# Spreading a rotary rotation over the next product's row tiles in the opening stage of an attention kernel

## The chip, the cores and the metric

The kernel runs on one core of a Trainium2 chip. The metric is the device time of one execution in microseconds (us); the time before is the median of three runs. TensorE (PE) multiplies matrices into PSUM, VectorE (DVE), ScalarE (ACT) and GpSimd (POOL) work on the results, and SyncE (SP) issues transfers. Each engine takes its own instructions in order and waits on semaphores.

## The reference, cut to what matters

For x of 1024 tokens by 512 channels:

```
xn = layernorm(x)
q, k, v = xn@wq + bq, xn@wk + bk, xn@wv + bv          # 32 query heads, 8 key/value heads, 16 wide
q, k = rope(q), rope(k)                                # rotary positions
s = softmax(q k^T / 4) v                               # each key/value head serves 4 query heads
z = xn@W^T + b;  m = sum_e p_e * (xn@A_e)@B_e          # dense part and low-rank part
gamma = min(0.5*|z| / (|m| + 1e-6), 1)
out = x + s * silu(z + gamma*m)
```

## The kernel before, in words

**Groups.** The attention runs as eight groups, one for each key/value head with its four query heads. The softmax subtracts a row maximum from each row of scores, so the maxima of group g+1 are found while group g is computed: in a group PE alternates a score tile for ACT's exponential (line 1501) with a row tile of the next group (`score_rows`, line 1369), and DVE reduces each row tile to its maximum (`row_max`, line 1081; 64 reductions in a group, 448 in all). Row tiles go round four PSUM banks (`sm`); tile n waits until DVE has read tile n-4. Every third score is followed by a block of P times V (line 1469), or, at the start of group 0, by half of a dense product (`dense3`, line 1442).

**The opening stage.** Group 0's own maxima come from 32 row tiles, numbered 0 to 31 here, each of two matmuls into two banks (`next_maximum`, line 1394). For each, ACT takes the relu of one bank (`first_relu`, line 849) and DVE adds the other and takes the maximum (`first_row_max`, line 1069). A tile waits until DVE has done the row maximum of the tile before the last (two banks each). These tiles are mixed into twelve products, in the order of the list `MIXED` (line 69): q(1,0), v1, q(1,1), u0, q(2,0), u1, q(2,1), z0, q(3,0), z1, q(3,1), z2, with the number of row tiles in each. Most products have two halves of six matmuls (line 1248); up to two row tiles stand after each half. Low-rank products m0 to m3 (line 1277) go ahead of the z. The loops of PE (line 1400), DVE (line 1126) and ACT (line 899) all walk `MIXED`.

**A rotation.** A query product q is rotated in five steps: DVE multiplies by the cosine (line 1047), exchanges the pairs of rows (the shuffle, line 1049) and multiplies by the sine (line 1051), in `rope`; POOL adds the two (`rope_sum`, line 591); ACT makes the high part (`cast`, line 820) and POOL the low part (`low_part`, line 595), which SP then puts in place. Before, DVE does its three after all the row maxima of that q, and ACT the cast ahead of the third relu of the next product (`r == 2`).

**Who frees a bank.** The products go round four banks, in the order of the list `PJ`; a product waits until the one four places before it has been read (`claim`, line 1223). A q's bank is free after its shuffle; a z's after DVE's `add_b` (line 1123); q(3,0) takes the bank of q(2,1). At the start of group 0 the first score takes the bank of q(3,1), and `dense3` the bank of z2 (`claim_bank`, lines 1439 and 1498).

**Other work of the stage.** ACT squares m and z for their norms (lines 865 and 876), POOL computes gamma (line 661), DVE adds gamma*m to z (`gate_sum`, line 1095), ACT takes the tanh (line 853) and DVE finishes the gate (`gate`, line 1101). ACT's `square_of_m(3)` waits for `gate(0)`. High and low parts of W^T, A and B are made by ACT, DVE (line 1110) and POOL on the way.

Of the kernel before, what the change touches and what calls it, by code (L numbers as in the profile page):

```python
# [23 lines left out]
F32 = mybir.dt.float32  # L24
# [5 lines left out]
P = 128  # L30
# [38 lines left out]
MIXED = [("q", (1, 0), 4), ("v", 1, 0), ("q", (1, 1), 4), ("u", 0, 3), ("q", (2, 0), 3), ("u", 1, 3), ("q", (2, 1), 3),  # L69
         ("z", 0, 3), ("q", (3, 0), 2), ("z", 1, 2), ("q", (3, 1), 2), ("z", 2, 3)]  # L70
# [8 lines left out]

for _kind, _i, _rows in MIXED:  # L80
    if _kind == "z":
        PJ += [("m", _i, "act")] + ([("m", _i + 1, "act")] if _i == 2 else [])
    PJ += [(_kind, _i, "act" if (_kind, _i) == ("u", 1) else "dve")]
    if (_kind, _i) == ("z", 0):
        PJ += [("max0", 0, "act")]
# [102 lines left out]
def build(nc, x, wq, wk, wv, biases, bv, wT, b, A, B, p_sc, cosT, sinT, ident, identb, ones, out):  # L188
    ctx = ExitStack()
    with ctx:  # L190
# [354 lines left out]
        def _(pool):  # L545
# [72 lines left out]

            rope_sum(0)
            for n in range(len(halves) - 2):  # L620
                low_part(n)
# [15 lines left out]
                if halves[n] == ("q", (1, 1)):  # L637
                    for k, c in enumerate((0, 1)):
                        pool.wait_ge(wT_high_done, 3 + k)
                        pool.tensor_tensor(by_columns(wT_low_parts[:, c, :]), by_columns(wT_sb[:, c, :]),  # L640
                                           wT_high(c).bitcast(F32), ALU.subtract).then_inc(wT_low_pool, 1)
                    pool.wait_ge(b_high_done, 1)
                    pool.tensor_tensor(b_low[:, :], B_sb[:, :], b_high[:, :].bitcast(F32),
                                       ALU.subtract).then_inc(b_low_done, 1)
# [13 lines left out]
            def gamma(t):  # L658

                pool.wait_ge(norm_done, 2 * t + (3 if t == 2 else 2))  # L660
                pool.tensor_tensor(gam[:, t, :], norms[:, t, :], consts[:, 1:2].broadcast_to((P, 2)),  # L661
                                   ALU.pow).then_inc(pow_step, 1)
                pool.wait_ge(pow_step, 4 * t + 1)
                pool.tensor_scalar(gam[:, t, 1:2], gam[:, t, 1:2], EPS_M, None, ALU.add).then_inc(pow_step, 1)
                pool.wait_ge(pow_step, 4 * t + 2)
                pool.tensor_tensor(gam[:, t, 1:2], gam[:, t, 1:2], consts[:, 2:3], ALU.pow).then_inc(pow_step, 1)
                pool.wait_ge(pow_step, 4 * t + 3)
                pool.tensor_tensor(gam[:, t, 0:1], gam[:, t, 0:1], gam[:, t, 1:2], ALU.mult).then_inc(pow_step, 1)
                pool.wait_ge(pow_step, 4 * t + 4)
                pool.tensor_scalar(gam[:, t, 0:1], gam[:, t, 0:1], C_CLAMP, 1.0, ALU.mult,  # L670
                                   ALU.min).then_inc(gamma_done, 1)

# [8 lines left out]
            gamma(0)  # L681
# [3 lines left out]
            pool.wait_ge(pj_dve, emptied(PJ_AT["v", 1])[1])  # L685
# [111 lines left out]
        def _(act):  # L797
# [100 lines left out]
            entry, waiting = 0, None  # L898
            for kind, i, rows in MIXED:
                if kind == "v":  # L900
                    cast(waiting)
                    waiting = None
# [3 lines left out]
                for r in range(rows):  # L906
                    if r == 2 and waiting is not None:
                        cast(waiting)
                        waiting = None
# [107 lines left out]
        def _(dve):  # L1017
# [17 lines left out]
            def rope(kind, i):  # L1035
# [647 lines left out]
```

## Time and profile before

| | |
|---|---|
| median of 3 runs | 427.78 us (427.43 to 428.59) |
| the profiled execution | 427.93 us, span 426.1 us, mean granted clock 0.986 |
| busy, share of the span | PE 96%, DVE 84%, ACT 78%, POOL 44% |
| opening stage with row tiles | about 36 to 97 us |
| groups 0 to 6 | 97 to about 375 us |
| last group and end | to 426 us |

A busy PE is no proof of a PE bound: its matmuls are pipelined, their ends are modelled, and PE can be paced by whoever empties its banks. So the views below are read for who waits for whom, and for the starts of instructions rather than for their ends.

### The profile page before, as it was taken

How to read it: one execution, taken by the hardware profiler on the slowest of the kernel's cores; microseconds unless marked ns; L12 is line 12 of the kernel's file. 1: busy time of each engine (PE TensorE's matmuls, PEld its weight loads, DVE VectorE, ACT ScalarE, POOL GpSimd, SP SyncE). 2: the span in 40 equal slices, each digit the busy share in tenths (PEclk: the TensorE clock that was granted, in tenths of full speed). 3: DMA queues.
4: the chain of work that ended last, by engine and by line, in shares of the span. 5: the costliest groups of instructions: out<-in, count | busy, mean ns of one | idle time of the engine just before them, and what ended most of it. 6: DMA issues, size and time to landing. Idle time of an engine off the chain costs nothing.

```text
span 426.1 us, 8603 instructions
## 1 busy us (share of the span) xinstructions
PE 410.3 (96%) x3215; PEld 195.0 (46%) x3215; DVE 356.6 (84%) x643; ACT 333.6 (78%) x653; POOL 189.2 (44%) x243
## 2 busy tenths in 40 slices
PE   7999989989999999999999999999999999999994
PEld 3556545655434344444444443444444343454441
DVE  5862677775999999999999999999999999933553
ACT  2445354574899998999989898999999999976884
POOL 7979972548444230403142043314332455501555
PEclk9999999995999999999999999999999999999999
DMA  8959995544610020000000000000000030002002
GB/s 263 306 119 127 130 135 75 77 75 75 190 37 3 0 58 3 3 3 0 3 2 4 1 3 3 2 4 0 4 2 3 1 102 2 4 2 88 25 22 68
DMA packets 15449, 21.51 MB, mean 50 GB/s; under 512 B 3328, under 2 KB 7712, under 8 KB 15408
## 3 DMA queue, kind: packets, MB, share of 16 engines
q1 hardware_dynamic: 13888, 19.85, 22.6%
q10 hardware_dynamic: 1520, 1.12, 1.0%
q8 instruction: 25, 0.41, 0.4%
q14 instruction: 16, 0.13, 0.1%
HBM read 10.13 MB, written 2.10 MB: 29 GB/s over the span
## 4 chain that ended last, share of the span: by engine, by line
PE 84%; POOL 6%; ACT 4%; DVE 3%; issue 2%; DMA 1%; DVEq 0%; ACTq 0%; POOLq 0%
PE st L1501 33%; PE oT L1469 27%; PE oT L1556 3%; PE sm L1581 3%; PE st L1248 2%; PE sm L1478 2%; PE oT L1248 2%; PE st L1535 2%; PE sm L1394 2%; PE sm L1369 1%; POOL arena L591 1%; PE oT L1442 1%; POOL x_low_parts L602 1%; DVE relus L1069 1%; POOL qA L595 1%
## 5 line engine op out<-in xcount | busy, mean ns | idle before, releaser
L1081 DVE TENSOR_REDUCE half_top<-sm 128x1 f32<-128x512 f32 x448 | 271.0, 680 | 4.2 <-PE sm L1369 3.6
L979 ACT ACTIVATE arena<-st 128x512 f32<-128x512 f32 x448 | 233.0, 600 | 25.4 <-PE st L1501 20.5
L1369 PE MATMUL sm<-kA,qA 48*128 48x512 f32 x448 | 157.4, 446 | 1.4 <-DVE row_top L1069 1.4
L1501 PE MATMUL st<-qA,kA 50*128 50x512 f32 x448 | 155.3, 442 | 0.1
L1469 PE MATMUL oT<-arena,vg 128*32 128x256 f32 (+3 forms) x1568 | 128.5, 419 | 0.1
L1501 PEld LDWEIGHTS st<-qA,kA 50*128 50x128 f32 x448 | 74.0, 186 | 97.7 <-ACT arena L979 80.8
L718 POOL TENSOR_TENSOR rsum<-junk,consts 128x16 f32<-128x16 f32 x13 | 37.9, 2915 | 101.2 <-ACT junk L947 101.2
L1369 PEld LDWEIGHTS sm<-kA,qA 48*128 48x128 f32 x448 | 74.0, 186 | 3.2 <-DVE row_top L1069 2.1
L1469 PEld LDWEIGHTS oT<-arena,vg 128*32 128x32 f32 x1568 | 33.5, 108 | 46.1 <-issue 42.5
L1069 DVE CUSTOM_DVE_ANT_0 relus<-sm,relus 128x512 f32<-128x512 f32 x32 | 21.4, 687 | 19.9 <-ACT relus L849 16.3
L1004 ACT ACTIVATE arena<-st 128x512 f32<-128x512 f32 x48 | 26.9, 601 | 9.4 <-PE st L1535 9.4
L613 POOL TENSOR_TENSOR maxp<-row_top,consts 128x16 bf16<-128x16 f32 x16 | 3.5, 216 | 60.9 <-DVE row_top L1088 60.9
L849 ACT ACTIVATE relus<-sm 128x512 f32<-128x512 f32 x32 | 18.0, 594 | 12.8 <-PE sm L1394 12.8
L1394 PE MATMUL sm<-k_first,qA 48*128 48x512 f32 x64 | 13.7, 469 | 4.1 <-DVE row_top L1069 3.9
L661 POOL TENSOR_TENSOR gam<-norms,consts 128x2 f32<-128x2 f32 x8 | 5.7, 715 | 26.9 <-DVE uT L1194 21.5
L591 POOL TENSOR_TENSOR arena<-arena 128x512 f32<-128x512 f32 x9 | 11.5, 1276 | 12.9 <-DVE arena L1051 12.9
L1556 PE MATMUL oT<-arena,vg 128*32 128x512 f32 x128 | 15.6, 599 | 1.0 <-ACT arena L1004 1.0
L820 ACT ACTIVATE arena<-arena 128x512 fp32r<-128x512 f32 x7 | 4.4, 629 | 13.2 <-POOL arena L591 13.2
L1535 PE MATMUL st<-qA,kA 50*128 50x512 f32 x48 | 12.7, 464 | 0.1
L1186 DVE TENSOR_TENSOR late_gate<-sm,b_sb 128x512 f32<-128x512 f32 x4 | 2.8, 692 | 11.2 <-PE sm L1581 11.2
L1394 PEld LDWEIGHTS sm<-k_first,qA 48*128 48x128 f32 x64 | 5.4, 184 | 14.2 <-DVE row_top L1069 7.7
L595 POOL TENSOR_TENSOR arena<-arena 128x512 fp32r<-128x512 f32 x7 | 9.0, 1286 | 5.5 <-ACT arena L820 5.5
(193 smaller groups left out, 483.0 us busy)
## 6 DMA issues: line engine op xcount, KB each, us to landing
qA<-arena SPq DMA_DIRECT2D x45, 128.0 KB, 4.6
x_sb<-in_x SPq DMA_DIRECT2D x16, 256.0 KB, 3.8
wT_sb<-in_wT SPq DMA_DIRECT2D x2, 1024.0 KB, 7.0
kA<-qA SPq DMA_DIRECT2D x12, 128.0 KB, 6.7
out<-x_sb SPq DMA_DIRECT2D x1, 896.0 KB, 4.3
out<-x_sb SPq DMA_DIRECT2D x4, 224.0 KB, 2.0
z_sb<-in_wq SPq DMA_DIRECT2D x1, 768.0 KB, 10.0
B_sb<-in_B SPq DMA_DIRECT2D x2, 256.0 KB, 7.1
```

What stands on the lines that cost most here:

```text
L718: pool.tensor_tensor(sums, came[:, :, :, D], consts[:, 2:3].unsqueeze(2).broadcast_to((P, TH, REP)), ALU.pow).then_inc(sums_inv, 1)
L849: act.activation(relus[:, e % 2, :], sm[:, 2 * e % 4, :], ACT.Relu).then_inc(relu_done, 1)
L979: act.activation(probs[:, s % PB, h, :], st[:, st_score(0, s, h) % 3, :], ACT.Exp, scale=float(D) ** -0.5).then_inc(st_free, 1)
L1004: act.activation(probs[:, s % PB, h, :], last_bank(last_score(s, k)), ACT.Exp, scale=float(D) ** -0.5).then_inc(last_free, 1)
L1069: return dve.tensor_tensor_reduce(relus[:, n % 2, :], bank, relus[:, n % 2, :], 1.0, LOWEST, ALU.add, ALU.max, to)
L1081: dve.tensor_reduce(half_top[:, e // 16, e % 16, j % 2:j % 2 + 1], sm[:, n % 4, :], AX.X, ALU.max).then_inc(sm_free, count)
L1369: pe.matmul(sm[:, n % 4, :], qA[rows, half, g // 2, h, qt * P:(qt + 1) * P], kA[rows, g // 2, kh * HALF:(kh + 1) * HALF], start=True, stop ...
L1394: pe.matmul(sm[:, n % 4, :], queries, k_first[kh * ROWS:kh * ROWS + KR, :], start=True, stop=True).then_inc(sm_full, 1)
L1469: mm = pe.matmul(oT[h * VC:(h + 1) * VC, cols], vg[:, g % 2, kt, :], probs[:, (NT * half + kt) % PB, h, cols], start=(kt == 0), stop=(kt = ...
L1501: pe.matmul(st[:, n % 3, :], kA[rows, g // 2, kt * P:(kt + 1) * P], qA[rows, half, g // 2, h, :], start=True, stop=True).then_inc(st_full, 1)
L1535: pe.matmul(last_bank(n), kA[rows, place, kt * P:(kt + 1) * P], qA[rows, half, place, h, :], start=True, stop=True).then_inc(last_full, 1)
L1556: mm = pe.matmul(oT[h * VC:(h + 1) * VC, :], vg[:, LAST % 2, s % NT, :], probs[:, s % PB, h, :], start=(s % NT == 0), stop=(s % NT == NT - 1))
```

## The change

Two row tiles move to the front: u0 and u1 get four instead of three, q(3,1) one instead of two and z2 two instead of three. DVE's three instructions of a rotation now stand in the next product of `MIXED`: the cosine after its first row maximum, the shuffle after its second, the sine after its third; what does not fit (fewer row tiles) follows its last row maximum. The rotation of q(1,0) stands in v1, which has no row tiles, as before. ACT's cast moves behind the relus of the product after that. The reading of v1's bank moves from DVE to ACT. DVE's `gate_sum(1)` and `add_b(2)` move from between the row maxima of z2 to behind the rotation of q(3,1). On POOL the low parts of W^T and B go ahead of `low_part` of q(1,1), and `gamma(0)` ahead of `low_part` of q(2,1).

```diff
-MIXED = [("q", (1, 0), 4), ("v", 1, 0), ("q", (1, 1), 4), ("u", 0, 3), ("q", (2, 0), 3), ("u", 1, 3), ("q", (2, 1), 3),
-         ("z", 0, 3), ("q", (3, 0), 2), ("z", 1, 2), ("q", (3, 1), 2), ("z", 2, 3)]
+MIXED = [("q", (1, 0), 4), ("v", 1, 0), ("q", (1, 1), 4), ("u", 0, 4), ("q", (2, 0), 3), ("u", 1, 4), ("q", (2, 1), 3),
+         ("z", 0, 3), ("q", (3, 0), 2), ("z", 1, 2), ("q", (3, 1), 1), ("z", 2, 2)]
...
-    PJ += [(_kind, _i, "act" if (_kind, _i) == ("u", 1) else "dve")]
+    PJ += [(_kind, _i, "act" if (_kind, _i) in (("u", 1), ("v", 1)) else "dve")]
...
             for n in range(len(halves) - 2):
+                if halves[n] == ("q", (2, 1)):
+                    gamma(0)
+                if halves[n] == ("q", (1, 1)):
+                    for k, c in enumerate((0, 1)):
...
                 low_part(n)
...
-            gamma(0)
             split(len(halves) - 2)
             gamma(1)
             split(len(halves) - 1)
-            pool.wait_ge(pj_dve, emptied(PJ_AT["v", 1])[1])
+            pool.wait_ge(pj_dve, emptied(PJ_AT["v", 0])[1])
+            pool.wait_ge(pj_act, emptied(PJ_AT["v", 1])[1])
...
-            entry, waiting = 0, None
+            entry, turning, waiting = 0, None, None
             for kind, i, rows in MIXED:
                 if kind == "v":
-                    cast(waiting)
-                    waiting = None
+                    act.wait_ge(pj_full, PJ_AT["v", i] + 1)
+                    act.activation(v_sb[:, i * TH:(i + 1) * TH, :],
+                                   pj(PJ_AT["v", i]).rearrange("p (t n) -> p t n", t=TH), ACT.Copy).then_inc(pj_act, 1)
+                    cast(turning)
+                    turning = None
...
                 for r in range(rows):
-                    if r == 2 and waiting is not None:
-                        cast(waiting)
-                        waiting = None
...
-                if kind == "q":
-                    waiting = halves.index((kind, i))
-                elif waiting is not None:
+                if waiting is not None:
                     cast(waiting)
-                    waiting = None
+                waiting = turning
+                turning = halves.index((kind, i)) if kind == "q" else None
...
+            cast(waiting)
...
-            def rope(kind, i):
+            def rope(kind, i, stages=range(3)):
...
-            gate_work = {("z", 1, 0): (gate_sum, 0), ("q", (3, 1), 0): (gate, 0), ("z", 2, 0): (gate_sum, 1)}
+            gate_work = {("z", 1, 0): (gate_sum, 0), ("q", (3, 1), 0): (gate, 0)}
...
-            n = 0
+            n, turning = 0, None
             for kind, i, rows in MIXED:
...
                 for r in range(rows):
-                    if (kind, i, r) == ("z", 2, 2):
-                        add_b(2)
                     first_row_max(n)
                     n += 1
+                    if turning is not None and r < 3:
+                        rope("q", turning, (r,))
...
-                if kind == "q":
-                    rope("q", i)
+                if turning is not None and rows < 3:
+                    rope("q", turning, range(rows, 3))
+                turning = i if kind == "q" else None
                 if (kind, i) == ("u", 0):
                     low_of_u()
-                if kind == "v":
-                    keep_values(i)
-                if kind == "z" and i != 2:
+                if kind == "z":
+                    if i == 2:
+                        gate_sum(1)
                     add_b(i)
```

## Rows read from the trace of the kernel before

**Rows 1.** The page's costliest groups: DVE's reductions of groups 0 to 6

```profile
L1081 DVE TENSOR_REDUCE half_top<-sm 128x1 f32<-128x512 f32 x448 | 271.0, 680 | 4.2 <-PE sm L1369 3.6
```

**Rows 2.** Timeline of DVE, 94 to 163 us (start, duration, engine, line, operation)

```profile
94.14 1.38 DVE L1095 SCALAR_TENSOR_TENSOR z_sb<-m_sb,gam,z_sb 128x512 f32<-128x512 f32 x1
...
96.05 0.68 DVE L1123 TENSOR_TENSOR z_sb<-oT,b_sb 128x512 f32<-128x512 f32 x1
...
97.26 1.87 DVE L1081 TENSOR_REDUCE half_top<-sm 128x1 f32<-128x512 f32 x3
101.83 1.89 DVE L1081 TENSOR_REDUCE half_top<-sm 128x1 f32<-128x512 f32 x3 [2.70 <-PE sm L1369]
105.51 0.69 DVE L1174 TENSOR_TENSOR z_sb<-oT,b_sb 128x512 f32<-128x512 f32 x1 [1.79 <-PE oT L1442]
106.27 1.89 DVE L1081 TENSOR_REDUCE half_top<-sm 128x1 f32<-128x512 f32 x3
...
143.46 19.33 DVE L1081 TENSOR_REDUCE half_top<-sm 128x1 f32<-128x512 f32 x32
```

**Rows 3.** Busy time by 1 us stretches: PE, PEld, DVE, ACT, POOL; granted clock; DMA

```profile
96.00:97.00 1.00, 0.73 (x4) 0.30 (x4) 1.00 (x4) 0.86 (x3) 1.00 (x2) 0.93 0.06 23
97.00:98.00 1.00, 0.61 (x1) 0.28 (x1) 1.00 (x4) 1.00 (x3) 0.84 (x3) 0.50 0.69 209
...
107.00:108.00 1.00, 1.00 (x11) 0.26 (x9) 1.00 (x2) 0.81 (x2) 0.00 (x0) 0.95 0.00 0
```

**Rows 4.** Waits of PE, 36 to 106 us: total, times, longest

```profile
PE sm L1394 <- DVE row_top L1069: 3.9, 5, 1.2
```

**Rows 5.** Timeline of PE in the opening stage: row tiles and halves of products

```profile
66.37 0.49 PE L1394 MATMUL sm<-k_first,qA 48*128 48x512 f32 x2 [0.53 <-DVE row_top L1069]
...
71.07 0.51 PE L1394 MATMUL sm<-k_first,qA 48*128 48x512 f32 x2
...
72.30 0.40 PE L1248 MATMUL oT<-wq_high,x_high_parts 128*128 128x512 f32 x1
...
73.76 0.73 PE L1394 MATMUL sm<-k_first,qA 48*128 48x512 f32 x4
74.42 0.50 PE L1248 MATMUL oT<-wT_high,x_high_parts 128*128 128x512 f32 x1
...
76.01 0.51 PE L1394 MATMUL sm<-k_first,qA 48*128 48x512 f32 x2
...
91.47 0.73 PE L1394 MATMUL sm<-k_first,qA 48*128 48x512 f32 x4
```

**Rows 6.** Timeline of DVE in the opening stage

```profile
45.44 0.68 DVE L1062 COPY v_sb<-st 128x512 f32<-128x512 f32 x1
49.20 0.69 DVE L1069 CUSTOM_DVE_ANT_0 relus<-sm,relus 128x512 f32<-128x512 f32 x1 [3.08 <-ACT relus L849]
...
65.53 0.68 DVE L1069 CUSTOM_DVE_ANT_0 relus<-sm,relus 128x512 f32<-128x512 f32 x1
...
72.38 0.69 DVE L1069 CUSTOM_DVE_ANT_0 relus<-sm,relus 128x512 f32<-128x512 f32 x1 [1.33 <-ACT relus L849]
...
72.99 0.74 DVE L1047 SCALAR_TENSOR_TENSOR arena<-st,bias,arena 128x512 f32<-128x512 f32 x1
...
74.43 0.75 DVE L1051 SCALAR_TENSOR_TENSOR arena<-arena,bias 128x512 f32<-128x512 f32 x1
```

**Rows 7.** Timeline of ACT in the opening stage

```profile
71.61 0.60 ACT L849 ACTIVATE relus<-sm 128x512 f32<-128x512 f32 x1 [1.43 <-PE sm L1394]
...
90.27 0.60 ACT L865 ACTIVATE junk<-st 128x512 bf16<-128x512 f32 x1 [0.36 <-PE st L1277]
...
92.39 1.10 ACT L849 ACTIVATE relus<-sm 128x512 f32<-128x512 f32 x2
```

**Rows 8.** Timeline of POOL, 93 to 97 us: sum and low part of q(3,1)

```profile
93.70 1.27 POOL L591 TENSOR_TENSOR arena<-arena 128x512 f32<-128x512 f32 x1 [2.39 <-DVE arena L1051]
95.71 1.28 POOL L595 TENSOR_TENSOR arena<-arena 128x512 fp32r<-128x512 f32 x1 [0.74 <-ACT arena L820]
```

More of the change, by code:

```diff
@@ L617, in maxima, with gamma @@
                                    ALU.subtract).then_inc(max_parts, 1)
+            def gamma(t):
+                pool.wait_ge(norm_done, 2 * t + (3 if t == 2 else 2))
+                pool.tensor_tensor(gam[:, t, :], norms[:, t, :], consts[:, 1:2].broadcast_to((P, 2)),
+                                   ALU.pow).then_inc(pow_step, 1)
+                pool.wait_ge(pow_step, 4 * t + 1)
+                pool.tensor_scalar(gam[:, t, 1:2], gam[:, t, 1:2], EPS_M, None, ALU.add).then_inc(pow_step, 1)
+                pool.wait_ge(pow_step, 4 * t + 2)
+                pool.tensor_tensor(gam[:, t, 1:2], gam[:, t, 1:2], consts[:, 2:3], ALU.pow).then_inc(pow_step, 1)
+                pool.wait_ge(pow_step, 4 * t + 3)
+                pool.tensor_tensor(gam[:, t, 0:1], gam[:, t, 0:1], gam[:, t, 1:2], ALU.mult).then_inc(pow_step, 1)
+                pool.wait_ge(pow_step, 4 * t + 4)
+                pool.tensor_scalar(gam[:, t, 0:1], gam[:, t, 0:1], C_CLAMP, 1.0, ALU.mult,
+                                   ALU.min).then_inc(gamma_done, 1)
             rope_sum(0)
             for n in range(len(halves) - 2):
+                if halves[n] == ("q", (2, 1)):
+                    gamma(0)
+                if halves[n] == ("q", (1, 1)):
+                    for k, c in enumerate((0, 1)):
+                        pool.wait_ge(wT_high_done, 3 + k)
+                        pool.tensor_tensor(by_columns(wT_low_parts[:, c, :]), by_columns(wT_sb[:, c, :]),
+                                           wT_high(c).bitcast(F32), ALU.subtract).then_inc(wT_low_pool, 1)
+                    pool.wait_ge(b_high_done, 1)
+                    pool.tensor_tensor(b_low[:, :], B_sb[:, :], b_high[:, :].bitcast(F32),
+                                       ALU.subtract).then_inc(b_low_done, 1)
                 low_part(n)
@@ L636, in _ @@
                     low_of_tokens(1)
[L637 to L644, printed above, removed]
                 if halves[n] == ("q", (2, 0)):
@@ L656, in split @@
                 low_part(n)
[L658 to L671, printed above, removed]
             def group_values(g):
@@ L1041, in rope @@
                 tok = slice(hh * HALF, (hh + 1) * HALF)
-                dve.wait_ge(pj_full, e + 1)
-                if n >= 2:
-                    dve.wait_ge(part2, n - 1)
-                if n == 4:
-                    dve.wait_ge(diff_done, 1)
-                dve.scalar_tensor_tensor(rotated_at(n), pj(e), bias[:, col, 0:1], cos_sb[:, tok],
-                                         ALU.add, ALU.mult).then_inc(cos_mul, 1)
-                dve.stream_shuffle(swp[:, n % 2, :], pj(e), PARTNER).then_inc(pj_dve, 1)
-                dve.wait_ge(pj_dve, emptied(e)[1])
-                dve.scalar_tensor_tensor(swp[:, n % 2, :], swp[:, n % 2, :], bias[:, col, 1:2], sin_sb[:, tok],
-                                         ALU.add, ALU.mult).then_inc(sin_mul, 1)
+                if 0 in stages:
+                    dve.wait_ge(pj_full, e + 1)
+                    if n >= 2:
+                        dve.wait_ge(part2, n - 1)
+                    if n == 4:
+                        dve.wait_ge(diff_done, 1)
+                    dve.scalar_tensor_tensor(rotated_at(n), pj(e), bias[:, col, 0:1], cos_sb[:, tok],
+                                             ALU.add, ALU.mult).then_inc(cos_mul, 1)
+                if 1 in stages:
+                    dve.stream_shuffle(swp[:, n % 2, :], pj(e), PARTNER).then_inc(pj_dve, 1)
+                if 2 in stages:
+                    dve.wait_ge(pj_dve, emptied(e)[1])
+                    dve.scalar_tensor_tensor(swp[:, n % 2, :], swp[:, n % 2, :], bias[:, col, 1:2], sin_sb[:, tok],
+                                             ALU.add, ALU.mult).then_inc(sin_mul, 1)
             dve.wait_ge(small_in, 64)
```

## The prediction

> **What bounds the kernel now.** Read first the page's costliest groups: DVE's 448 reductions stand idle for 4.2 us in all [rows 1]. In the middle of the run 32 of them take 19.33 us without a gap, 0.604 us each [rows 2]. So from the first reduction to the last, DVE sets the pace; PE looks busy because it waits in line for DVE's banks. What happens before counts by two things: when this train of reductions starts (97.26), and the gaps in its first 10 us. These are 2.70 and 1.79 us [rows 2], the first when PE computes the first half of `dense3`, the second when DVE waits for its second half. I take as yardstick the seventh reduction, at 106.27 [rows 2]; what it is shifted by, the end is shifted by.
>
> Then the granted clock: 2.4 GHz up to 96, 0.93 of it in the stretch to 97, 0.50 (the 1.2 GHz level) from 97 to 107 and back at 107 to 108 [rows 3]. PE's busy share ahead of the fall was 0.73 and 0.61 of a stretch, with waits for row maxima between [rows 3]. That is why the two halves of `dense3` leave DVE idle.
>
> Last the waits of the opening stage: row tiles waited five times for a row maximum, 3.9 us in all, 1.2 at the longest [rows 4].
>
> **Prices.** From one profiled execution: a row maximum occupies DVE 0.61 us (72.38 to 72.99), cosine and shuffle together 1.44 (72.99 to 74.43), so 0.67 and 0.77, and the sine 0.67 like the cosine [rows 6]. A row maximum can start 1.31 us after its tile (71.07 to 72.38), 0.77 of it after the start of its relu (71.61) [rows 5 to 7]. A waiting tile starts 0.84 after the row maximum that lets it go (65.53 to 66.37) [rows 5, 6]. Half a product takes 1.46 us after another matmul (72.30 to 73.76) and 1.59 after row tiles (74.42 to 76.01); two row tiles take 0.66, one about 0.45 [rows 5]. Two squares of m with their copies hold ACT 2.12 us (90.27 to 92.39) [rows 7]. A POOL sum takes 1.27 us and the low part can start 0.74 after it [rows 8].
>
> **Part 1: v1's copy goes to ACT.** Worth nothing. DVE made it at 45.44, and then stood idle for 3.08 us until a relu at ACT; ACT had been waiting for a cast [rows 6]. The Trainium skill (Perfetto Trace Analysis, Optimizing Scalar/DVE Operations) says that moving work from DVE to ScalarE may pay where DVE is saturated; by it the sum would be 0.7 us lower. DVE isn't saturated there, so the row decides.
>
> **Part 2: u0 to q(2,1), rotations between row tiles.** I replayed the new orders of PE, DVE and ACT with the prices above, from tile 7 on (nothing before it changes). Row maximum 8 no longer waits for a whole rotation, so tile 10 starts at 54.9 rather than after the longest of those waits (1.2). But row maximum 9 now stands behind the cosine, and tile 11 waits 0.8 us for it. Tile 13 waits for row maximum 11, which has shuffle, sine and a low part of W^T ahead of it: 1.0. The same twice more around u1, where DVE's row maxima 15 to 18, the rotation and the second low part of W^T are one unbroken stretch of 5.2 us: tile 18 waits 0.9, tile 20 1.05. Together 3.75 us, where about 2.6 of the old 3.9 us lie in this stretch (one wait lies ahead of it, one in z2) [rows 4], and some 0.4 more inside pairs of tiles. So the waits move and don't shrink. z0's first row tile starts at 74.65; before, at 73.76 [rows 5]. It is 0.9 us later, with two more tiles done. The two tiles that are then missing further down save 0.66 us as a pair and about 0.9 apart [rows 5], so this part alone is about even.
>
> **Part 3: q(3,0) waits for a bank.** It takes the bank of q(2,1), free after the shuffle. Before, the shuffle was done ahead of z0's row maxima. Now it follows row maximum 23: that is row maximum 22 at 75.95, cosine, row maximum 23, shuffle from 77.8 to 78.6. PE has finished z0 and the transposed maxima by 77.5, and waits 1.15 us. Everything behind it in PE's order (m1, z1) waits too. `add_b(0)` comes after the sine, at 79.9, so ACT's square of z0 and the relus behind it go late, which makes DVE idle but doesn't hold PE again.
>
> **Part 4: z1 to z2.** z1's first tile at 84.6, q(3,1)'s at 88.35, z2's first tile at 93.2; before 91.47 with one tile fewer done [rows 5], so 1.7 us later. `gate_sum(0)` meets no POOL operation now and takes about 0.75 us like the sine; `gate_sum(1)` took 1.38 because POOL's sum had started at 93.70, ahead of it at 94.14 [rows 2, 6, 8]. On the other side, `gate(0)` after row maximum 29 now starts just behind POOL's low part of q(3,0), which follows the cast that ACT makes behind relu 29. I count about 1 us for it, since the bounds are 0 and a whole 1.28 [rows 8] and the replay has POOL first by only 0.2. ACT's square of m3 waits for that gate, and relu 30 for both squares: 95.4 rather than 94.4.
>
> **Part 5: the end of the stage.** Before, the train of reductions followed the last row maximum at once; `gate_sum(1)` and `add_b(2)` were done earlier [rows 2]. Now row maximum 30 is at 96.15, cosine, row maximum 31 at 97.45, shuffle at 98.05, sine at 98.8, `gate_sum(1)` at 99.5, `add_b(2)` at 100.15: the train starts at **100.8, 3.5 us later**. PE finishes z2 at 95.5 and then waits for q(3,1)'s shuffle, whose bank the first score takes, until 98.9. It does three scores with their row tiles (0.7 us) and waits again until 100.85 for `add_b(2)`, whose bank `dense3` takes. ACT's exponentials stand behind the last cast, at about 101.2; PE needs the first of them only behind `dense3`'s first half, so this costs nothing. SP gets its last transfers some 5 us later; what needs them is four score rows on, and the other POOL moves lie ahead of nothing that is late.
>
> **Part 6: the clock at the start of group 0.** PE now idles 4.65 us of the 5.35 from 95.5 to 100.85, more than ahead of the old fall [rows 3]. I take it that the clock falls again and is at 1.2 GHz for `dense3`. Then: three reductions ready at once to 102.6; first half of `dense3` 2.85 us as before (half the speed), the fourth reduction at 104.55, a gap of 1.95 (2.70 before); second half to 108.1, gap 1.9 (1.79); seventh reduction at 109.0. Against 106.27 that is **2.7 us later**, 0.8 of the 3.5 won back in the gap. The bounds of this part: with the clock at 2.4 GHz throughout, `dense3`'s halves take 1.4 us, the gaps shrink to 0.3, and the seventh reduction comes at 105.3, 1.0 us earlier than before; with the low clock lasting 3 us longer, PE does 3 us of work in 1.5 us more: 4.2 later.
>
> **Sum.** 0 (part 1) + 0.9 (part 2, at z0's first tile) + 1.0 (part 3, at z1's: 84.6 where the old order replays to 82.7) - 0.2 (part 4, at z2's: one tile fewer on the way) + 1.8 (part 5: from there to the train 7.6 us, before 5.8) - 0.8 (part 6) = 2.7. The profiled execution took 427.93 us; 430.6 on that scale. It stands 0.15 above the median of 427.78, so I say 430.5.
>
> **The rivals.**
> *The rotation fits into DVE's gaps (faster).* The Trainium skill (Perfetto Trace Analysis, Optimizing Scalar/DVE Operations) says that where Vector isn't saturated but causes bubbles on other engines, breaking up instructions may let work complete sooner, which is what this change does. By rows: DVE waited 1.33 us for relu 19 [rows 6], and a stage of 0.67 to 0.77 in such a gap is free. If the tiles come so far apart that all stages fall into gaps, the 3.75 us of waits in part 2 and 1.15 of part 3 are gone; the clock still falls. 2.7 - 4.9 = -2.2: 425.6. It decides at DVE between tiles 8 and 20: whether a stage starts before the next tile's relu is done. Against it: after the u tiles the same gap also has to take the low part of W^T. Chance 0.16.
> *The clock stays up.* -1.0: 426.8, within 0.3%. For it: PE has no other long wait from 79 to 95. Against it: the idle time above. Chance 0.10.
> *Half of it.* The waits of part 2 and 3 are half hidden (-2.45): 428.1, no change to be seen. Chance 0.10.
> *The low clock lasts longer.* 432.0. Chance 0.08.
> That the change does little of what it says can be for q(3,0) and q(3,1): z1 and z2 have two row tiles, so the third instruction stands behind the last one anyway; this is in parts 4 and 5.
>
> **How the numbers follow.** A measurement can tell about 0.3% (1.3 us) from no change. The forecast itself has 0.56. Slower: 0.56 + 0.08 = 0.64; same: 0.20; faster: 0.16. The range goes from 426.5 (most of the clock rival, not the faster one) to 432.3 (the longer low clock); about 0.2 is left out. The forecast's own range is 429.2 to 431.8: 1 us less if `gate(0)` goes ahead of POOL, 1.3 more for small delays in the replay.
>
> **What would show it.** Right: the first reduction near 100.8, straight behind `add_b(2)`, which follows the sine and `gate_sum(1)`; PE's first score of group 0 waiting some 3 us for a shuffle; q(3,0)'s first matmul waiting about 1 us for a shuffle; row tiles 11, 13, 18 and 20 waiting for row maxima; a clock of 0.50 in the stretches from 98 to about 108. Wrong: a train that starts before 98, or a clock of 1.00 throughout; either takes the forecast down to no change or below.

## The result and the profile of the changed kernel

The changed kernel takes **430.3 us** (median of 17 runs, 427.44 to 432.21), the kernel before 427.78 (17 runs, 423.65 to 430.22). The ratio is 1.0078, 95% interval 1.0052 to 1.0103: slower by 0.8%. 430.5 was forecast.

The number alone hides one thing: in both kernels the mean granted clock of a run is spread as well as its time, so the low TensorE clock seems to last longer in some executions than in others. Beside medians I therefore compare runs of the same mean clock. At 0.988 or less the kernel before has 428.38 (15 of 35 runs made with the first experiments), the changed one 430.8 (13 of its 17); at 0.989 to 0.995 they have 426.10 (15) and 427.93 (4). The change costs 2.4 and 1.8 us there.

This comparison is rough, in three ways. The experiments were run in three sets on three chips, each beside runs of the kernel before, whose median at 0.989 to 0.995 is 426.10, 426.98 and 426.47 in them: a difference below 1 us between sets tells little. The mean clock also counts a low stretch that every profile has at the end of the run. In the profile of the two row tiles alone (below; mean 0.994) the clock stays at 1.00 at the start of group 0, even while PE idles, and is low only from 418 us on (columns as in [rows 3]):

```profile
97.00:98.00 1.00, 0.00 (x0) 0.00 (x0) 1.00 (x2) 1.00 (x3) 0.31 (x1) 1.00 0.03 8
...
421.00:422.00 1.00, 0.00 (x0) 0.00 (x0) 0.20 (x1) 0.00 (x0) 0.00 (x0) 0.50 0.62 229
```

And it leaves out what an edit does to the clock itself: 13 of the 17 runs of the changed kernel have 0.988 or less, but 3 of 12 with q(3,1)'s rotation put back and none of 6 with all of them. So I also compare profiles whose low stretch at the start of group 0 has the same length.

The profiled execution of the changed kernel is one of the few of the second kind: 428.61 us, span 426.8, clock 0.994.

First the page's costliest groups, which answer to [rows 1]:

```profile
L1088 DVE TENSOR_REDUCE half_top<-sm 128x1 f32<-128x512 f32 x448 | 270.9, 679 | 2.8 <-PE sm L1378 2.2
...
L1510 PE MATMUL st<-qA,kA 50*128 50x512 f32 x448 | 153.7, 439 | 3.8 <-DVE arena L1055 3.7
```

PE's waits from 36 to 106 us, which answer to [rows 4]:

```profile
PE st L1510 <- DVE arena L1055: 3.7, 1, 3.7
PE sm L1403 <- DVE row_top L1076: 3.1, 5, 0.8
PE st L1257 <- DVE arena L1055: 1.1, 1, 1.1
PE oT L1451 <- DVE z_sb L1130: 1.0, 1, 1.0
```

The reductions stand idle less than before (2.8 us against 4.2), and yet the kernel is slower. PE has three waits that it did not have: for the shuffle of q(3,1) (L1055, ahead of the first score, L1510), for the shuffle of q(2,1) (ahead of q(3,0), L1257), and for `add_b(2)` (ahead of `dense3`, L1451). PE's timeline gives their places:

```profile
59.99 0.50 PE L1403 MATMUL sm<-k_first,qA 48*128 48x512 f32 x2 [0.58 <-DVE row_top L1076]
...
70.45 0.50 PE L1403 MATMUL sm<-k_first,qA 48*128 48x512 f32 x2 [0.59 <-DVE row_top L1076]
...
79.17 0.50 PE L1257 MATMUL st<-x_high_parts,wq_high 128*128 128x512 f32 x1 [1.08 <-DVE arena L1055]
...
99.38 0.46 PE L1510 MATMUL st<-qA,kA 50*128 50x512 f32 x1 [3.67 <-DVE arena L1055]
...
101.34 0.79 PE L1451 MATMUL oT<-wq_high,x_high_parts 128*128 128x512 f32 x1 [1.00 <-DVE z_sb L1130]
```

The end of the stage in DVE's timeline, which answers to [rows 2]:

```profile
93.06 1.65 DVE L1108 SCALAR_TENSOR_TENSOR z_sb<-m_sb,z_sb 128x512 f32<-128x512 f32 x1
96.62 0.69 DVE L1076 CUSTOM_DVE_ANT_0 relus<-sm,relus 128x512 f32<-128x512 f32 x1 [1.92 <-ACT relus L851]
...
97.90 0.68 DVE L1076 CUSTOM_DVE_ANT_0 relus<-sm,relus 128x512 f32<-128x512 f32 x1
...
99.27 0.75 DVE L1058 SCALAR_TENSOR_TENSOR arena<-arena,bias 128x512 f32<-128x512 f32 x1
99.94 0.74 DVE L1102 SCALAR_TENSOR_TENSOR z_sb<-m_sb,gam,z_sb 128x512 f32<-128x512 f32 x1
100.61 0.68 DVE L1130 TENSOR_TENSOR z_sb<-oT,b_sb 128x512 f32<-128x512 f32 x1
101.20 1.88 DVE L1088 TENSOR_REDUCE half_top<-sm 128x1 f32<-128x512 f32 x3
104.84 1.89 DVE L1088 TENSOR_REDUCE half_top<-sm 128x1 f32<-128x512 f32 x3 [1.76 <-PE sm L1378]
106.86 0.69 DVE L1183 TENSOR_TENSOR z_sb<-oT,b_sb 128x512 f32<-128x512 f32 x1
107.47 5.46 DVE L1088 TENSOR_REDUCE half_top<-sm 128x1 f32<-128x512 f32 x9
```

All of DVE is late by what stands in front of the train of reductions: row maximum 30 (96.62), cosine, row maximum 31 (97.90), shuffle, sine (99.27), `gate_sum(1)`, `add_b(2)`, and only then the first reduction (101.20). This profile began its opening stage 0.96 us later (first row maximum at 40.06, before at 39.10; the change touches nothing up to there). Counted from the first row maximum, the train starts at 61.14, before at 58.16: **3.0 us later**. The two first row maxima, before and now:

```profile
39.10 0.69 DVE L1069 CUSTOM_DVE_ANT_0 relus<-sm,relus 128x512 f32<-128x512 f32 x1 [3.58 <-ACT relus L849]
```

```profile
40.06 0.69 DVE L1076 CUSTOM_DVE_ANT_0 relus<-sm,relus 128x512 f32<-128x512 f32 x1 [3.57 <-ACT relus L851]
```

The clock, in one-us windows (columns as in [rows 3]):

```profile
100.00:101.00 1.00, 0.35 (x4) 0.00 (x0) 1.00 (x3) 0.00 (x0) 0.89 (x1) 0.98 0.02 8
101.00:102.00 1.00, 0.66 (x2) 0.56 (x3) 1.00 (x3) 0.15 (x1) 0.81 (x1) 0.50 0.00 0
...
104.00:105.00 1.00, 1.00 (x7) 0.55 (x6) 0.16 (x1) 0.74 (x3) 0.92 (x4) 0.81 0.72 197
```

It falls behind PE's 4.7 us of waiting, as forecast, but in this execution it stays low for only 3.4 us, where before it was low for 10 [rows 3]. So the gaps behind the third and sixth reduction are short here (1.76 and next to none, against 2.70 and 1.79), and the seventh reduction, my yardstick, comes at 67.41 against 67.17. From that seventh reduction to the end the device takes 321.1 to 321.7 us in every profile of this case, both kernels and all twelve experiments: the yardstick holds, and the time of every profiled execution is decided ahead of it.

### The profile page after: what moved, and what is told of

It reads as the page before. It is cut to its first block, busy times and chain, and to the rows that moved or that the text cites. A ratio compares the mean times of both kernels' runs of the same rounds, so it can differ in the third digit from the quotient of the medians.

```text
span 426.8 us, 8602 instructions
## 1 busy us (share of the span) xinstructions
PE 407.2 (95%) x3214; PEld 193.3 (45%) x3215; DVE 353.2 (83%) x642; ACT 334.7 (78%) x654; POOL 190.3 (45%) x243
## 4 chain that ended last, share of the span: by engine, by line
PE 78%; POOL 7%; DVE 5%; ACT 3%; issue 3%; DMA 2%; SPq 1%; DVEq 0%; ACTq 0%; POOLq 0%
PE st L1510 32%; PE oT L1478 27%; PE oT L1565 3%; PE sm L1590 3%; DMA x_sb<-in_x 2%; PE sm L1487 2%; PE st L1257 2%; PE sm L1378 2%; PE st L1544 2%; DVE relus L1076 2%; PE sm L1403 1%; POOL x_low_parts L602 1%; POOL arena L591 1%; PE oT L1451 1%; ACT relus L851 1%
## 5 line engine op out<-in xcount | busy, mean ns | idle before, releaser
L1510 PE MATMUL st<-qA,kA 50*128 50x512 f32 x448 | 153.7, 439 | 3.8 <-DVE arena L1055 3.7
L1378 PE MATMUL sm<-kA,qA 48*128 48x512 f32 x448 | 155.6, 442 | 0.0
L1510 PEld LDWEIGHTS st<-qA,kA 50*128 50x128 f32 x448 | 73.4, 184 | 100.8 <-ACT arena L983 81.8
L1244 PE MATMUL oT<-xT_sb,arena 128*128 128x512 f32 x24 | 11.2, 601 | 0.0
```

Of the source, the lines that this page charges most:

```text
L1378: pe.matmul(sm[:, n % 4, :], qA[rows, half, g // 2, h, qt * P:(qt + 1) * P], kA[rows, g // 2, kh * HALF:(kh + 1) * HALF], start=True, stop ...
L1510: pe.matmul(st[:, n % 3, :], kA[rows, g // 2, kt * P:(kt + 1) * P], qA[rows, half, g // 2, h, :], start=True, stop=True).then_inc(st_full, 1)
```

## The experiments

My theory: the rotations' new places cost the time, above all where PE waits for a bank that a shuffle gives back (q(2,1), q(3,1)) and where POOL blocks `gate(0)`; the clock falls because PE waits there. Rivals: the other parts of the change (two row tiles moved, v1's copy on ACT, casts one product later), or the clock alone. "At the same clock" means the medians at a mean clock of 0.988 or less / of 0.989 to 0.995, and "train" the first reduction counted from the first row maximum (before 58.16, changed 61.14).

### One rotation or gate put back at a time

**q(3,1)'s rotation** right behind its own product's row maximum (line at the end of DVE's loop over `MIXED`):

```diff
                 turning = i if kind == "q" else None
+                if kind == "q" and i in ((3, 1),):
+                    rope("q", i)
+                    turning = None
```

> The changed kernel, with the whole rotation of q(3,1) back behind that product's row maximum (after the gate) instead of among the row maxima of z2. Theory (the end of the stage: last rotation, gate sum and bias stand between the last row maximum and the first reduction): DVE was idle 1.9 us there, the rotation fits in, the first reduction comes at about 99.4 instead of 101.2 of the changed kernel's profile, PE's 3.7 us wait for the shuffle becomes under 1 us; time 1.5 to 2 us below the changed kernel's 430.3, about 428.5. Rival (only the clock's fall counts, and PE idles here either way): within 0.5 us of 430.3. Rival (the cost sits further up, in the row tiles): the same, no change.

Measured: 426.64 us, ratio to the kernel before 1.0007 (0.9974 to 1.0039); at the same clock 429.25 / 427.0, that is 1.6 / 0.9 below the changed kernel. Train at 59.31, 1.8 earlier. PE's waits:

```profile
PE sm L1381 <- DVE row_top L1076: 0.8, 1, 0.8
PE st L1513 <- DVE arena L1055: 0.5, 1, 0.5
```

The 3.7 us wait of the first score falls to 0.5, but 0.8 comes up behind it: PE waits next for the row maxima that are still to come. Of the 3.7 us the train got back 1.8, half. The profile has the low clock for 3.4 us, as the changed kernel's has, and its seventh reduction comes at 65.58, also 1.8 earlier. The median fell by more (3.7 us, below the 428.5 expected), because fewer runs had the long low clock.

**q(2,1)'s rotation**, the same edit with `(2, 1)`.

> The changed kernel, with the whole rotation of q(2,1) back behind that product's row maxima instead of among those of z0. Theory (q(3,0) waits for the bank that q(2,1)'s shuffle frees): PE's 1.1 us wait ahead of q(3,0) goes, DVE makes the rotation in 2.0 us of idle time ahead of row maximum 22, everything behind comes 1.1 us earlier; about 429.2. Rival (the end of the stage waits for ACT's squares anyway): the 1.1 us are eaten further down, within 0.3 us of 430.3.

Measured: 428.24, ratio 1.0036 (1.0008 to 1.0064); at the same clock 429.3 / 426.91, 1.5 / 1.0 below the changed kernel. The wait ahead of q(3,0) is gone from PE's list, the train starts at 59.95: 1.2 earlier for a wait of 1.1. Here the whole wait passed to the end, since everything behind q(3,0) stands in PE's order.

**`gate(0)`** ahead of row maximum 29 rather than behind it:

```diff
-            gate_work = {("z", 1, 0): (gate_sum, 0), ("q", (3, 1), 0): (gate, 0)}
+            gate_work = {("z", 1, 0): (gate_sum, 0)}
...
                 for r in range(rows):
+                    if (kind, i, r) == ("q", (3, 1), 0):
+                        gate(0)
                     first_row_max(n)
```

> The changed kernel, with the gate of tile 0 ahead of row maximum 29 instead of behind it. Theory (the gate met POOL's low part and took 1.65 us, and ACT's square of m3 and the last relus waited for it): the gate is done by 92.4 in DVE's idle time, the squares run through, relu 30 comes 1.05 us earlier and so does the first reduction; about 429.2. Rival (the 1.65 us are hidden behind other work): no change, 430.3.

Measured: 427.68, ratio 1.0039 (1.001 to 1.0069); at the same clock 429.68 / 427.05, 1.1 / 0.9 below. Train at 59.96. ACT's square of m3 and relu 30 come 1.2 us earlier, and the first score's wait falls from 3.7 to 2.6.

**The two early rotations**, q(1,1) and q(2,0), the same edit with both.

> The changed kernel with the rotations of q(1,1) and q(2,0) whole again, right behind their own product's row maxima; q(2,1), q(3,0), q(3,1) and all else stay as changed. Theory (part 2 of the prediction: waits only move, about even): within 0.5 us of the changed kernel at the same mean granted clock (430.8 where it is at most 0.988, 427.9 at 0.989 to 0.995), and the first reduction again about 61 us behind the first row maximum, because the end of the stage sets it. Rival (the scattered stages of the early stretch cost): 1 us or more below the changed kernel at the same clock. Other rival (they fit into DVE's gaps and gain): 1 us or more above it.

Measured: 429.61, ratio 1.0057 (1.0029 to 1.0085); at the same clock 429.88 / 427.88: 0.9 / 0.05 below the changed kernel, with a train 0.5 us *later* (61.69). That later train is not the rotations' doing. The profile (mean clock 0.982) has a low stretch from 58 to 62 us that no other profile of this case has:

```profile
59.00:60.00 1.00, 1.00 (x5) 0.50 (x4) 1.00 (x3) 0.08 (x1) 0.84 (x1) 0.50 0.01 4
```

Up to row maximum 21 this kernel has the same order as the one with all rotations put back (next section), and yet that row maximum comes 34.32 us behind the first, there 33.24: the low stretch cost 1.1. The changed kernel, at full clock, has it at 33.71, so the two scattered rotations cost 0.5 us. Part 2 of the change is thus about even. The same profile also caught the long low clock at the start of group 0, and so shows what the changed kernel's own profile doesn't. DVE, and one window:

```profile
100.96 1.87 DVE L1088 TENSOR_REDUCE half_top<-sm 128x1 f32<-128x512 f32 x3
104.81 1.89 DVE L1088 TENSOR_REDUCE half_top<-sm 128x1 f32<-128x512 f32 x3 [1.98 <-PE sm L1381]
108.49 0.69 DVE L1186 TENSOR_TENSOR z_sb<-oT,b_sb 128x512 f32<-128x512 f32 x1 [1.79 <-PE oT L1454]
```

```profile
108.00:109.00 1.00, 1.00 (x6) 0.52 (x6) 0.51 (x1) 0.00 (x0) 0.92 (x2) 0.50 0.89 100
```

With the clock at 0.50 from 100 to 109, the gap behind the third reduction is 1.98 us and the one ahead of `dense3`'s sum 1.79. I had forecast 1.95 and 1.9.

### All rotations put back

The same edit with all five. What is left of the change: two row tiles moved, v1's copy on ACT, casts one product later, POOL's order, `gate_sum(1)` and `add_b(2)` behind z2.

> The changed kernel with every rotation from q(1,1) to q(3,1) whole again, right behind its own product's row maxima. What is left of the change: the casts one product later, POOL's order, v1's copy on ACT, two row tiles moved to the front, gate_sum(1) and add_b(2) behind z2. Theory (the place of the rotations is the loss): about 0.5 us above the kernel before at the same mean granted clock, so 428.9 at most 0.988 and 426.6 at 0.989 to 0.995; the first score's wait of 3.7 us falls below 1. Rival (the later casts and POOL's order cost as much): 1.5 us or more above it, 429.9 and 427.6.

Measured: **423.2 us, ratio 0.9902 (0.9874 to 0.993)**, and at a clock of 0.989 to 0.995 423.35 against 426.47 before in the same session. Theory and rival both missed: rather than a remainder above the kernel before there is a gain of 3.1 us below it, and the place of the rotations costs 4.6 (423.35 against 427.93 at the same clock; the train starts at 56.46 rather than 61.14, 4.7 earlier). The change is a gain and a larger loss in one. This profile has the low clock for 3.4 us too:

```profile
96.21 1.87 DVE L1088 TENSOR_REDUCE half_top<-sm 128x1 f32<-128x512 f32 x3
...
102.60 5.46 DVE L1088 TENSOR_REDUCE half_top<-sm 128x1 f32<-128x512 f32 x9
```

Its seventh reduction comes 62.85 us behind the first row maximum, 4.6 earlier than the changed kernel's. The loss of 4.7 in the train can be parted: 0.5 for q(1,1) and q(2,0), 1.2 for q(2,1) and 1.8 for q(3,1), as above. q(3,0)'s rotation was not put back by itself, but between row maxima 28 and 29 only its place differs from the run with q(2,1) put back, and that run takes 4.15 us there, this one 3.08: another 1.1, together 4.6.

The gain lies in the train, 1.7 us earlier than in the kernel before. How much the gaps behind it add depends on the clock: against the profile of the kernel with only v1's copy moved (next section), whose clock is low for 3.4 us as well, the gap behind the third reduction is 1.49 rather than 2.37 and the seventh reduction 2.2 earlier. So the gain is 2.2 by these profiles and 3.1 by the medians. Where the train's part is from can be read when this kernel's ACT is laid beside that of the kernel in which only the tiles are moved (next section). That one first, PE's timeline at u0's row tiles and ACT's:

```profile
56.97 1.11 PE L1394 MATMUL sm<-k_first,qA 48*128 48x512 f32 x4 [1.18 <-DVE row_top L1069]
```

```profile
57.69 0.63 ACT L820 ACTIVATE arena<-arena 128x512 fp32r<-128x512 f32 x1 [2.07 <-POOL arena L591]
58.23 0.62 ACT L913 ACTIVATE b_high_parts<-B_sb 128x512 fp32r<-128x512 f32 x1
58.75 1.06 ACT L849 ACTIVATE relus<-sm 128x512 f32<-128x512 f32 x2
```

Then this one, PE and ACT again:

```profile
56.74 1.11 PE L1406 MATMUL sm<-k_first,qA 48*128 48x512 f32 x4 [1.20 <-DVE row_top L1076]
```

```profile
55.24 0.63 ACT L916 ACTIVATE b_high_parts<-B_sb 128x512 fp32r<-128x512 f32 x1
57.27 1.21 ACT L851 ACTIVATE relus<-sm 128x512 f32<-128x512 f32 x2 [1.41 <-PE sm L1406]
```

PE does the tiles at the same time in both, 16.97 and 16.99 us behind the first row maximum (40.00 and 39.75). In the old order ACT's cast (L820) waits 2.07 us for POOL's sum, with `b_high` and the relus of two tiles in line behind it, and the relus start 18.75 behind the first row maximum. With the cast one product later they wait for their tiles alone and start at 17.52: 1.2 us earlier, and DVE's row maxima and PE's next tiles with them. POOL's sum itself starts at the same time in both (16.39 and 16.40), so that here the place of the cast counts and not POOL's order. The same thing happens again at u1 (a cast that waits 1.85 for POOL in the old order). In all, ACT waited for POOL's sums 12.6 us in 5 casts before, and 3.9 in 2 in this kernel:

```profile
ACT arena L820 <- POOL arena L591: 12.6, 5, 5.9
```

```profile
ACT arena L822 <- POOL arena L591: 3.9, 2, 2.4
```

3.5 of that difference is the first cast (5.9 to 2.4), ahead of which ACT now copies v1; the run of that copy alone shows that it is worth nothing.

### The other parts by themselves, from the kernel before

**The two row tiles**: `MIXED` as in the change, and for z2's two tiles

```diff
-                    if (kind, i, r) == ("z", 2, 2):
+                    if (kind, i, r) == ("z", 2, 1):
                         add_b(2)
```

> The kernel before, with the new numbers of row tiles alone (u0 and u1 four, q(3,1) one, z2 two; the bias of z2 is added ahead of the last row maximum as before). Rotations, casts, POOL's order and v1's copy as before. Theory (the place of the rotations makes the change slower, the two tiles are about even): within 0.8 us of the kernel before at the same granted clock (428.4 at 0.986, 426.1 at 0.99 to 0.995). Rival (the two tiles moved to the front are what costs): 1.5 to 2.5 us above it at the same clock.

Measured: 426.16, ratio 0.9994 (0.9961 to 1.0027); at the same clock 429.22 / 425.9, the kernel before in that session 428.51 / 426.98. No difference that can be told; the train starts at 58.63, 0.5 later than before.

**v1's copy on ACT**, with ACT's instruction as in the change and DVE's `keep_values` left out:

```diff
-    PJ += [(_kind, _i, "act" if (_kind, _i) == ("u", 1) else "dve")]
+    PJ += [(_kind, _i, "act" if (_kind, _i) in (("u", 1), ("v", 1)) else "dve")]
```

> The kernel before, with the copy of v1's bank moved from DVE to ACT and nothing else. Theory (DVE waits 3.1 us behind it for a relu that waits for a cast, and ACT is idle): no change, within 0.4 us of the kernel before at the same clock. Rival (moving work off DVE pays): 0.6 us less.

Measured: 426.53, ratio 0.9982 (0.9951 to 1.0013); 428.26 / 425.81. No difference that can be told, and the train starts at 58.14, where it did before (58.16). This profile, of a kernel that can't be told from the one before, has the low clock for 3.4 us (98 to 101.4), where that of before has 10:

```profile
104.27 5.47 DVE L1085 TENSOR_REDUCE half_top<-sm 128x1 f32<-128x512 f32 x9
```

Its seventh reduction comes at 65.05 behind the first row maximum, so at the same low clock the changed kernel's (67.41) is 2.4 us late.

So neither brings the train forward, and the 1.7 us of the kernel with all rotations put back are left to the later casts, POOL's order and the two sums behind z2. The rows above speak for the casts, but none of these three was run by itself.

### The clock by itself

Matmuls whose result nobody reads fill PE's wait ahead of the first scores; nothing is left out. In the changed kernel 16 of them:

```diff
+            def fill(count):
+                claim(4 + PJ_AT["m", 2])
+                for _ in range(count):
+                    pe.matmul(st[:, PJ_AT["m", 2] % 4, :], x_high[:, 0, 0, 0:P], wT_high(0), start=True, stop=True)
...
                 pe.wait_ge(stacked[n], 16 * SLOT_DMAS)
+            fill(16)
```

> The changed kernel, with 16 matmuls that nobody reads put on PE, into a bank that is free, where it waits for the last shuffle ahead of group 0 (some 3.5 us of work in a wait of 3.7). Theory (the fall of the clock to 1.2 GHz in the first half of the dense product costs what the profile's gap shows): the clock stays at 2.4 GHz through group 0's start in nearly all runs, mean clock 0.995 or above, first reduction at the same place (101.2), seventh reduction at about 105.5; about 427.3, with little spread. Rival (the clock falls for another reason, or the filling doesn't count): clock 0.986 in most runs, 430.3.

Measured: 427.23, ratio 1.0021 (0.9997 to 1.0044), mean clock 0.996 or more in all 12 runs. The train starts where it did (61.03, before the filling 61.14), and the gap behind the third reduction falls to 0.51:

```profile
100.00:101.00 1.00, 0.69 (x3) 0.60 (x4) 1.00 (x3) 0.19 (x1) 0.78 (x1) 1.00 0.00 0
```

**In the kernel before**, 2 ahead of its last row tile and 5 ahead of the first scores:

> The kernel before, with 7 matmuls that nobody reads on PE where it waits: two ahead of row tile 31, five between z2 and group 0. Theory (waits ahead of group 0 are what lets the clock fall; at 2.4 GHz the gaps in the first reductions shrink): mean clock 0.996 or above in most runs, about 425.0, which is what the kernel before shows in its runs at that clock; 2 us below its median of 427.2. Rival (these waits are too short to fill, the filling delays group 0): clock as before, 427.5 to 428.

Measured: **424.28, ratio 0.9935 (0.9907 to 0.9963)**, again 0.996 or more in all 12 runs, train at 58.19 (58.16):

```profile
97.38 1.88 DVE L1081 TENSOR_REDUCE half_top<-sm 128x1 f32<-128x512 f32 x3
```

So the low clock costs the changed kernel 3.1 us (430.3 to 427.23) and the kernel before 3.5 (427.78 to 424.28), and with a full clock in both the change still costs 2.95 us (427.23 against 424.28). The two are from different sets, but their profiles agree: the trains lie 2.8 apart (61.03 and 58.19), the seventh reductions 3.0 (66.55 and 63.55). The clock is not what the two kernels differ by; the train is.

### Put together

**Four edits in the changed kernel**: q(2,1) and q(3,1) put back, `gate(0)` first, and 6 filling matmuls.

> The changed kernel with the rotations of q(2,1) and q(3,1) back behind their own row maxima, the gate of tile 0 ahead of row maximum 29, and six filling matmuls ahead of group 0. Theory (the three costs add up, each in its own place): first reduction 4 us earlier than in the changed kernel's profile, 1.1 us earlier than in the kernel before; clock 0.996 or above; about 423.5, below the kernel before at any clock. Rival (they overlap: each waits for the same squares at ACT): 425 to 426.

Measured: **423.27, ratio 0.9913 (0.9884 to 0.9942)**, train at 57.67. That is 3.5 earlier than in the changed kernel, where the three moves by themselves add up to 4.2, so they overlap a little.

**And `gate_sum(1)` out of the way**, behind the third reduction, with POOL's use of its result held back for it:

```diff
                 if kind == "z":
-                    if i == 2:
-                        gate_sum(1)
                     add_b(i)
...
+                    if first and j == 2:
+                        gate_sum(1)
...
+                if t == 2:
+                    pool.wait_ge(gate_in, 2)
```

> The version with all four edits that beat both kernels (423.27), with the gate sum of z2 moved from ahead of the first reduction to behind the third one of group 0, and add_b(2) straight behind the row maxima. In that version this sum took 1.59 us, of which DVE stood blocked while POOL's sum was in flight, and nothing needs it until z2's gate. Theory (everything ahead of the first reduction shifts the end): the first reduction comes about 1.5 us earlier, and the time falls by 1 to 1.5 us, to about 422. Rival (the first scores or the exponentials are the later ones, so DVE waits there instead): no change, 423.3.

Measured: **422.25, ratio 0.989 (0.9859 to 0.9922)**: 1.0 us less, and 1.1 at a clock of 0.996 or more (422.15 against 423.23). The fastest of the kernels here; next come the one with all rotations put back and the one with four edits (423.2 and 423.27). DVE without and with the move:

```profile
97.61 1.59 DVE L1102 SCALAR_TENSOR_TENSOR z_sb<-m_sb,gam,z_sb 128x512 f32<-128x512 f32 x1
...
99.72 1.87 DVE L1088 TENSOR_REDUCE half_top<-sm 128x1 f32<-128x512 f32 x3
```

```profile
94.53 0.69 DVE L1132 TENSOR_TENSOR z_sb<-oT,b_sb 128x512 f32<-128x512 f32 x1
95.29 1.89 DVE L1090 TENSOR_REDUCE half_top<-sm 128x1 f32<-128x512 f32 x3
97.09 1.05 DVE L1104 SCALAR_TENSOR_TENSOR z_sb<-m_sb,gam,z_sb 128x512 f32<-128x512 f32 x1
98.07 1.87 DVE L1090 TENSOR_REDUCE half_top<-sm 128x1 f32<-128x512 f32 x3
```

The train starts 1.4 us earlier (56.28). In its new place the sum still holds DVE for a microsecond, but POOL holds it up less there (1.05 us rather than 1.59; it took 0.74 in the changed kernel, where POOL was idle when it began), and the gap of 0.42 that stood behind the third reduction pays a part. At the seventh reduction 1.1 us are left (61.47 against 62.61).

**The same move in the kernel before with its filled clock**:

> The kernel before with matmuls that fill PE's idle time ahead of the first scores (424.28), and the gate sum of z2 moved behind the third reduction of group 0; rotations where the kernel before has them. Theory (what stands ahead of the first reduction shifts the end): DVE is freed of 1.4 us ahead of its first reduction, so about 1 us less, 423.3. Rival (ahead of the first reduction DVE then waits for scores or for the last row maximum): no change, 424.3.

Measured: 423.99 against 424.28, ratio to the kernel before 0.9917 (0.989 to 0.9944). The rival holds: 0.3 us rather than 1. What is late there instead is the last row maximum, whose relu stands behind q(3,1)'s cast, which waits for POOL:

```profile
95.67 0.63 ACT L822 ACTIVATE arena<-arena 128x512 fp32r<-128x512 f32 x1 [1.55 <-POOL arena L591]
96.20 0.58 ACT L851 ACTIVATE relus<-sm 128x512 f32<-128x512 f32 x1
```

```profile
96.96 0.69 DVE L1071 CUSTOM_DVE_ANT_0 relus<-sm,relus 128x512 f32<-128x512 f32 x1 [0.87 <-ACT relus L851]
```

It is the same kind of wait as at u0 and u1 above, here at the end of the stage.

## Why the prediction came out right

The time (430.5 against 430.3) and the sign are right, and the mechanism is the one forecast. Term by term; positions set against a forecast are those of the changed profile less its 0.96, times in brackets stand as in the profile:

- **Part 1**, 0: right, by the run of its own. ACT itself stood there at a cast that waited 5.9 us for POOL's sum.
- **Part 2**, about even: right, within the 0.5 us found above. Its waits were mis-sized: tiles 11, 13, 18 and 20 (56.88, 59.99, 67.35, 70.45) waited 0.57 to 0.59 each, 2.3 in all, not 3.75. Two prices were too high: a waiting tile starts 0.74 behind its row maximum (59.25 to 59.99), not 0.84, and a shuffle between two row maxima holds DVE for 0.62 (56.76 to 57.38), not 0.77. That is 0.1 to 0.25 of each wait; where the rest comes from I did not follow. z0's first tile came at 74.2, not at 74.65.
- **Part 3**, 1.15 for q(2,1)'s shuffle: 1.08, and worth 1.2 by its run.
- **Part 4**, 1 us for `gate(0)` blocked by POOL: right. It ran 1.65 us (93.06) where it takes 0.69 unblocked, and putting it first was worth 1.2 of the train. The Trainium skill (SBUF — State Buffer, Who interferes with whom) says that a Vector instruction with two SBUF inputs contends with a GpSimd instruction that reads SBUF, and that whoever is first blocks the other; these rows agree, with POOL's low part first by 0.19. The gate before, then POOL's low part now:

```profile
90.21 0.69 DVE L1101 SCALAR_TENSOR_TENSOR z_sb<-m_sb,z_sb 128x512 f32<-128x512 f32 x1
```

```profile
92.87 1.29 POOL L595 TENSOR_TENSOR arena<-arena 128x512 fp32r<-128x512 f32 x1 [1.06 <-ACT arena L822]
```

- **Part 5**, train at 100.8: 100.24, so 3.0 later and not 3.5, because z0 to z2 came 0.4 to 0.8 earlier than replayed. The waits were 3.67 and 1.0, where 3.4 and 1.25 were forecast.
- **Part 6**: that the clock falls is right; how long it stays low is not settled by the kernel alone. I took the ten us at 0.50 of the one profile of before as the rule. In a long one (that of the run with the early rotations put back) the gaps are those forecast. In the changed kernel's own profile the seventh reduction is only 0.24 us late against that long one of before, but 2.4 late against the profile with the same 3.4 us (v1's copy alone): 3.0 from the train, less 0.6 won back in the gap behind the third reduction (1.76 against 2.37). Forecast were 3.5 and 0.8.
- **The sum**, 2.7: measured 2.5 between the medians, 2.4 and 1.8 at the same clock. Its total was right, in part by luck, since the misses of parts 5 and 6 partly cancel, and its parts were not told apart. The new places of the rotations cost 4.6 us and the rest gains 2.2 to 3.1; the rows point to the casts, which no longer hold up relus. My working has no term for those casts: part 5 names only the last of them, as costing nothing, and what they gain went unseen into the replay of part 2 to 4. It could have been read before: ACT's 12.6 us of waiting for POOL's sums stand in no row that I took.

Of the rivals, *the rotation fits into DVE's gaps* fell: scattered early the stages gained nothing, scattered late they cost. The rule cited there from the Trainium skill (Perfetto Trace Analysis, Optimizing Scalar/DVE Operations), that breaking up instructions may let work complete sooner, is not borne out here, where the piece that frees a bank (the shuffle) completes later by being split off. What helped was a whole instruction moved to where its input is ready. *The clock stays up* did not happen in the profile, but its price was about right: 426.8 forecast, 427.23 with the clock held up by filling. *The low clock lasts longer* (432.0): its time is found in single runs, but not its cause. The slowest, 432.21, has a mean clock of 0.986, as has one of 428.52.

Open: the casts, POOL's order and the two sums behind z2 by themselves, the shuffle moved without the rest of its rotation, and why the clock comes back sooner in some executions.

## What to carry to other kernels

When an instruction sequence is broken up among other work, look first for the piece that frees a buffer or that another engine waits for: moving whole rotations among the next product's maxima, the shuffles that free banks with them, cost more (4.6 us) than all the rest of this change gained (2.2 to 3.1), and putting them back gives 423.2 us. An in-order engine should not take up an instruction that waits for another engine while finished work stands in line behind it; a product later the casts at u0 and u1 waited for nothing. And part a change into its pieces before the verdict on it: this one is slower by 0.8%, and with one part of it undone faster by 1%.

## What the runs showed of the hardware that I had not expected

- The stretch at 1.2 GHz at the start of group 0 is 10.2 us long in the profile of before, 3.4 in that of a kernel that can't be told from it (v1's copy alone), and missing in that of the two row tiles alone, though PE idled there for 1.8 us on end. Each kernel was profiled once; that the length varies between executions of one kernel is argued from the mean clocks (0.982 to 0.994 in the changed kernel's 17 runs). Time goes with them (before: 428.4 us at a mean clock of 0.988 or less, 426.1 at 0.989 to 0.995, 425.0 at 0.996 and more), but not all of its spread: the changed kernel's runs at 0.986 alone reach from 428.52 to 432.21. With PE's wait filled by 7 matmuls, the spread falls from 6.3 us (423.83 to 430.11, 34 runs) to 1.5 (423.65 to 425.14, 12 runs).
- Executions of kernels that are alike up to there reach their first row maximum between 39.0 and 42.05 us after the start. The experiment with four edits shows the latest (42.05) in its profile, and that one run took 425.83 us, where its median is 423.27. I did not follow where this comes from.
